# Attention with a routed expert layer on one core: the preparation reordered, with unread products on TensorE ahead of the first x

## The reference

```python
q, k, v = (split_heads(x @ W) for W in (Wq, Wk, Wv))
attn = softmax(q @ k.T * 128 ** -0.5) + bias        # bias[h, s, s]: rows of rel_table, clipped at both ends
out = (attn @ v) over the heads
x = layernorm(x + (norm(out, eps=1e-3) * gamma + beta))
w = softmax(top4((x @ hasher_w.T) @ keys.T))
x = layernorm(x + (x + scale * sum_k w_k * (silu(x @ values_down[k]) @ values_up[k])))
```

## Time and profile before

| what | us |
|---|---|
| median of 3 runs | 302.32 |
| lowest and highest | 301.48 and 304.64 |
| span of the profiled execution | 303.0 |
| PE busy in it | 280.6 (93%) |
| DVE, ACT, POOL busy | 235.2, 197.8, 129.1 |

### The profile page before, as it was taken

The page is one execution under the profiler, slowest core; times in us unless marked ns, Lnnn a source line. Parts: engine busy times, 40 slices in busy tenths (PEclk is TensorE's granted clock), DMA queues, the critical chain, the costliest instruction groups (busy, mean ns, idle before and its releaser), DMA issues.

```text
span 303.0 us, 10998 instructions
## 1 busy us (share of the span) xinstructions
PE 280.6 (93%) x4664; PEld 147.6 (49%) x4665; DVE 235.2 (78%) x517; ACT 197.8 (65%) x390; POOL 129.1 (43%) x212
## 2 busy tenths in 40 slices
PE   4969999999999989999999999999999999888991
PEld 3545434444444344444557554445566545375481
DVE  4755989998999978987787799977886863067854
ACT  3731389686777667789864876888566689921710
POOL 8576134110104651127556321288464033873641
PEclk9996999999999999999999999999999999999998
DMA  5566057355042302000403030006000000010011
GB/s 156 163 164 150 0 142 126 74 146 148 2 112 52 80 4 82 4 2 22 140 6 80 6 80 5 3 5 183 12 4 4 4 5 3 0 39 2 0 37 35
DMA packets 18574, 17.27 MB, mean 57 GB/s; under 512 B 6830, under 2 KB 16222, under 8 KB 18526
## 3 DMA queue, kind: packets, MB, share of 16 engines
q1 hardware_dynamic: 17856, 16.39, 21.3%
q10 hardware_dynamic: 670, 0.19, 0.3%
HBM read 12.18 MB, written 4.23 MB: 54 GB/s over the span
## 4 chain that ended last, share of the span: by engine, by line
PE 68%; DVE 11%; DMA 6%; ACT 5%; POOL 4%; issue 3%; SPq 1%; POOLq 0%; DVEq 0%
PE sm_ps L1208 16%; PE st_ps L1208 14%; PE ov_ps L1263 13%; PE mi_ps L1208 6%; PE si_ps L1208 5%; DVE neg_max L919 5%; DMA k_stack<-parts_dram 3%; ACT probs L773 2%; PE mi_ps L1270 1%; DVE stats L958 1%; POOL rstd L505 1%; ACT w_rows L675 1%; PE si_ps L1288 1%; PE st_ps L1435 1%; PE st_ps L1520 1%
## 5 line engine op out<-in xcount | busy, mean ns | idle before, releaser
L919 DVE TENSOR_REDUCE neg_max<-sm_ps 128x1 f32<-128x512 f32 x256 | 166.4, 686 | 31.3 <-PE sm_ps L1208 24.6
L773 ACT ACTIVATE probs<-st_ps 128x512 f32<-128x512 f32 x256 | 138.0, 608 | 33.8 <-PE st_ps L1208 33.8
L1208 PE MATMUL sm_ps<-k_stack,q_stack 96*32 96x512 bf16 x984 | 97.1, 383 | 2.8 <-DVE neg_max L919 2.1
L1208 PE MATMUL st_ps<-q_stack,k_stack 128*32 128x512 bf16 x1024 | 88.7, 380 | 0.2 <-ACT probs L773 0.2
L1263 PE MATMUL ov_ps<-probs,v_cur 128*32 128x256 f32 x1024 | 76.3, 378 | 0.0
L1208 PEld LDWEIGHTS sm_ps<-k_stack,q_stack 96*32 96x32 bf16 x984 | 26.3, 94 | 50.3 <-DVE neg_max L919 33.6
L519 POOL TENSOR_TENSOR hid<-hid,w_rows 128x512 f32<-128x512 f32 x27 | 34.2, 1281 | 30.8 <-ACT w_rows L675 30.7
L1263 PEld LDWEIGHTS ov_ps<-probs,v_cur 128*32 128x32 f32 x1024 | 31.6, 110 | 22.7 <-ACT probs L773 0.4
L1208 PEld LDWEIGHTS st_ps<-q_stack,k_stack 128*32 128x32 bf16 x1024 | 27.7, 96 | 28.4 <-ACT probs L773 9.2
L982 DVE SCALAR_TENSOR_TENSOR hid<-tanh_sb,mi_ps 128x512 f32<-128x512 f32 x24 | 16.3, 681 | 15.0 <-ACT tanh_sb L810 15.0
L1208 PE MATMUL mi_ps<-x_t,down_sb 128*32 128x512 f32 x192 | 25.1, 592 | 0.0
(11 more groups left out here) (183 smaller groups left out, 301.3 us busy)
## 6 DMA issues: line engine op xcount, KB each, us to landing
q_stack<-parts_dram SPq DMA_DIRECT2D x16, 288.0 KB
k_stack<-parts_dram SPq DMA_DIRECT2D x48, 96.0 KB
parts_dram<-parts SPq DMA_DIRECT2D x24, 128.0 KB, 2.4
x_sb<-L_attn_x SPq DMA_DIRECT2D x4, 256.0 KB, 4.7
out<-y_out SPq DMA_DIRECT2D x3, 256.0 KB, 2.3
down_sb<-L_ffn_values_down SPq DMA_DIRECT2D x1, 512.0 KB, 5.7
up_sb<-L_ffn_values_up SPq DMA_DIRECT2D x1, 512.0 KB, 8.0
rel_win<-rel_dram SPq DMA_DIRECT2D x1, 256.0 KB, 2.8
```

The source lines that it names most:

```text
L773: nc.scalar.activation(probs[:, u % 2, j, :], st_ps[:, score_bank(u * J + j), :], ACT.Exp, scale=SCORE_SCALE).then_inc(probs_ready, 1)
L919: nc.vector.tensor_reduce(neg_max[:, g % 2, col:col + 1], sm_ps[:, c % 2, :], AX.X, ALU.max, negate=True).then_inc(max_ready, 1)
L1208: i = nc.tensor.matmul(dst[n * TILE:(n + 1) * TILE], weights[:, n * TILE:(n + 1) * TILE], moving, **flags)
```

## The change

A new tile `warm` is filled by POOL's first instruction, ahead of `ident`. PE begins with products of it that nobody reads: five pairs (`row_halves`), each of two matmuls of 64 rows by 128 columns against 512 columns in float32r, one on the upper and one on the lower half of the rows and into two banks of `st_ps`, and two sets of four bf16 matmuls of 32 columns against 512 (`tiled`). The order is three pairs, then twice a set and a pair.

SP issues Wq and Wk behind x of batch 0, then x of 1, Wv, x of 2 and 3. The load of `rel_win` moves behind the six writes of batch 0's parts, and beta behind `load_shift(0, 0)`. ACT copies batch 1's turned x after the parts of batch 0. All four `add_beta` move to round 0, behind POOL's low parts of batch 3. PE makes q and k of batch 0 ahead of the turn of batch 1, v of batch 0 behind that turn, and the constant part of the bias, then the hasher's product, ahead of the first products for the maxima; the four of these that stood between the constant part's products are no longer there, so that two and twelve are made up to the end of the bias pieces and four more behind them.

```diff
--- before.py
+++ after.py
@@ -7,7 +7,7 @@
                                           hasher_w, keys, values_down, values_up, ffn_scale, out):
 
 
-    F32, BF16 = mybir.dt.float32, mybir.dt.bfloat16
+    F32, BF16, F32R = mybir.dt.float32, mybir.dt.bfloat16, mybir.dt.float32r
     ALU, ACT, AX = mybir.AluOpType, mybir.ActivationFunctionType, mybir.AxisListType
 
     B, S, E = x.shape
@@ -59,6 +59,7 @@
 
 
         ident, ident_bf = sb("ident", [P, P]), sb("ident_bf", [P, P], BF16)
+        warm = sb("warm", [P, P + S], F32R)
         minus_half = sb("minus_half", [P, C])
         wq_sb, wk_sb, wv_sb = sb("wq_sb", [P, E]), sb("wk_sb", [P, E]), sb("wv_sb", [P, E])
         gamma_sb, beta_sb = sb("gamma_sb", [P, E]), sb("beta_sb", [P, E])
@@ -118,6 +119,7 @@
         rel_dram = nc.dram_tensor("rel_dram", [NWIN + P // H, H], F32, kind="Internal").ap()
 
         waits_met = sem("waits_met")
+        warm_set = sem("warm_set")
         consts_made, stack_set, rows_cleared = sem("consts_made"), sem("stack_set"), sem("rows_cleared")
         x_loaded = [sem(f"x_loaded{b}") for b in range(B)]
         rows_loaded, beta_loaded = sem("rows_loaded"), sem("beta_loaded")
@@ -384,16 +386,12 @@
                 sp.dma_start(x_sb[:, b], x[b].rearrange("(c p) e -> p c e", p=P)).then_inc(x_loaded[b], 16)
 
             load_x(0)
-            load_x(1)
             sp.dma_start(wq_sb[:], w_q).then_inc(proj_loaded[0], 16)
             sp.dma_start(wk_sb[:], w_k).then_inc(proj_loaded[1], 16)
+            load_x(1)
+            sp.dma_start(wv_sb[:], w_v).then_inc(proj_loaded[2], 16)
             load_x(2)
             load_x(3)
-            sp.dma_start(wv_sb[:], w_v).then_inc(proj_loaded[2], 16)
-            sp.dma_start(beta_sb[:], bass.AP(beta.tensor, 0, [[0, P], [1, E]])).then_inc(beta_loaded, 16)
-            sp.wait_ge(rel_written, 32)
-            sp.dma_start(rel_win[:], bass.AP(rel_dram.tensor, 0, [[H, P], [H * P, NWIN // P], [1, P]])) \
-              .then_inc(rel_loaded, 16)
 
             def write_parts(b, *written):
 
@@ -408,6 +406,9 @@
                         sp.dma_start(rows[i], parts[:, b, a, i]).then_inc(written[a % len(written)], 16)
 
             write_parts(0, *first_written)
+            sp.wait_ge(rel_written, 32)
+            sp.dma_start(rel_win[:], bass.AP(rel_dram.tensor, 0, [[H, P], [H * P, NWIN // P], [1, P]])) \
+              .then_inc(rel_loaded, 16)
             sp.wait_ge(stack_set, 1)
             sp.wait_ge(rows_cleared, 1)
             sp.wait_ge(first_written[0], PARTS * 16)
@@ -417,6 +418,7 @@
             for g in range(1, G):
                 load_slice(0, g)
             load_shift(0, 0)
+            sp.dma_start(beta_sb[:], bass.AP(beta.tensor, 0, [[0, P], [1, E]])).then_inc(beta_loaded, 16)
             sp.dma_start(gamma_sb[:], bass.AP(gamma.tensor, 0, [[0, P], [1, E]])).then_inc(rows_loaded, 16)
             sp.dma_start(scale_sb[:], bass.AP(ffn_scale.tensor, 0, [[0, P], [1, 1]])).then_inc(rows_loaded, 16)
             write_parts(1, parts_written[1])
@@ -540,6 +542,7 @@
                         .then_inc(low_made, 1)
 
 
+            nc.gpsimd.memset(warm[:].bitcast(F32), 1.0).then_inc(warm_set, 1)
             nc.gpsimd.memset(ident[:], 0.0).then_inc(consts_made, 1)
             pool.wait_ge(consts_made, 1)
             nc.gpsimd.affine_select(out=ident[:], in_=ident[:], compare_op=ALU.not_equal, fill=1.0, base=0,
@@ -568,15 +571,11 @@
                 nc.gpsimd.tensor_tensor(x_sb[:, b], x_sb[:, b], beta_sb[:].unsqueeze(1).to_broadcast([P, C, E]),
                                         ALU.add).then_inc(xb_ready, 1)
 
-            pool.wait_ge(beta_loaded, 16)
-            add_beta(0)
-            add_beta(1)
             low_parts(1)
             low_parts(2)
             pool.wait_ge(v_copied, B)
             for g in range(G):
                 fetch_values(0, g)
-            add_beta(2)
             for i in range(PARTS):
                 rows = slice(i * NE, (i + 1) * NE)
                 pool.wait_ge(consts_made, 8)
@@ -585,12 +584,10 @@
                 nc.gpsimd.tensor_copy(spread[rows], ident[rows, rows].rearrange("r (j n) -> r j n", j=FJ).unsqueeze(3)
                                       .to_broadcast([NE, FJ, NJ, PD])).then_inc(spread_made, 1)
             pool.wait_ge(spread_made, PARTS)
-            add_beta(3)
             split_shift(0, 0)
             for n, a in enumerate((1, 0)):
                 pool.wait_ge(last_copied, n + 1)
                 nc.gpsimd.tensor_sub(resid[:, 1, a], resid[:, 1, a], parts[:, B - 1, a, 0, :]).then_inc(last_resid, 1)
-
             def round_(t, attention, experts, more, late):
                 f = t - 1
                 if attention and not is0(t):
@@ -605,6 +602,9 @@
                     split_shift(t, 1)
                 if is0(t):
                     low_parts(B - 1)
+                    pool.wait_ge(beta_loaded, 16)
+                    for b in range(B):
+                        add_beta(b)
                 if experts:
                     norm(f, "a", EPS_ATTENTION, z[:], z[:]).then_inc(pool_step, 1)
                     pool.wait_ge(pool_step, pool_at(f, "ascale"))
@@ -699,9 +699,9 @@
             nc.scalar.dma_start(rel_dram[LAST + 1:, :], bass.AP(rel_table.tensor, LAST * H,
                                                                 [[0, NWIN + P // H - LAST - 1], [1, H]])).then_inc(rel_written, 16)
             x_copy(0)
-            x_copy(1)
             high_parts(0)
             middle_parts(0)
+            x_copy(1)
             x_copy(2)
             x_copy(3)
             high_parts(1)
@@ -1397,17 +1397,29 @@
                 if kc == C - 1 and piece == pieces - 1:
                     i.then_inc(bias_mm, 1)
 
+            def row_halves():
+
+                for half in range(2):
+                    rows = slice(half * (P // 2), (half + 1) * (P // 2))
+                    nc.tensor.matmul(st_ps[:, half, :], warm[rows, 0:P], warm[rows, P:], start=True, stop=True)
+
+            pe.wait_ge(warm_set, 1)
+            for n in range(3):
+                row_halves()
+            for n in range(2):
+                tiled(st_ps[:, 2, :], warm[:].bitcast(BF16)[:, 0:P], warm[:].bitcast(BF16)[:, P:P + S], start=True, stop=True)
+                row_halves()
             pe.wait_ge(consts_made, 2)
             turn_x(0)
-            turn_x(1)
             pe.wait_ge(proj_loaded[0], 16)
             make_qk(0, 0)
             pe.wait_ge(proj_loaded[1], 16)
             make_qk(0, 1)
+            turn_x(1)
+            pe.wait_ge(proj_loaded[2], 16)
+            make_v(0)
             turn_x(2)
             turn_x(3)
-            pe.wait_ge(proj_loaded[2], 16)
-            make_v(0)
             make_qk(1, 0)
             make_qk(1, 1)
             make_v(1)
@@ -1423,11 +1435,7 @@
             make_v(3)
             pe.wait_ge(keys_loaded, 32)
             turn(si_ps[0:PD, 0:NE], keys_sb[:], ident[0:NE, 0:NE]).then_inc(table_mm, 1)
-            pe.wait_ge(xt_copied, B)
-            early_maxima(2)
-            pe.wait_ge(table_copied, 2)
-            nc.tensor.matmul(si_ps[:, 0:NE], hasher_sb[:], keys_t[:], start=True, stop=True).then_inc(table_mm, 1)
-
+            pe.wait_ge(table_copied, 1)
             pe.wait_ge(v_copied, B)
             pe.wait_ge(high_made, 6)
             pe.wait_ge(resid_made, 6)
@@ -1435,8 +1443,11 @@
                 i = nc.tensor.matmul(st_ps[:, 2, 0:CG * J * B * D], rel_t[:, LAST:LAST + P],
                                      v_all[:, kc, 0:CG * J].rearrange("p h b d -> p (h b d)"),
                                      start=(kc == 0), stop=(kc == C - 1))
-                early_maxima(1)
             i.then_inc(bias_mm, 1)
+            pe.wait_ge(table_copied, 2)
+            nc.tensor.matmul(si_ps[:, 0:NE], hasher_sb[:], keys_t[:], start=True, stop=True).then_inc(table_mm, 1)
+            pe.wait_ge(xt_copied, B)
+            early_maxima(2)
             for kc in range(C):
                 bias_product(CG, kc)
                 early_maxima(1, product=tiled)
```

## The result

The changed kernel took 305.11 us in the median of 11 runs (302.44 to 305.83), beside 302.32 (300.66 to 304.64) for 11 runs of the kernel before on the same chip: a ratio of 1.0066, 95% interval 1.0034 to 1.0099. It is slower by 0.3 to 1.0%; the forecast was 298.1.

The account below looks back on a forecast made before the run. It took a row of waits in the preparation, up to POOL's first split at 34.74, as the bound. Split 4.2 earlier, nothing lost in round 0: span 303.0 - 4.2 = 298.8, time 302.3 - 4.2 = 298.1 us, range 296.7 to 300.9.

Parts of the forecast that it names:

- the base: Starting point of the sum: the profile's span of 303.0, taken as 0.7 above the median of 302.32.
- split: POOL's first split, the mark on which everything up to the first scores hangs: 30.5 forecast for 34.74.
- Unread products: PE's start: seven steps end at 4.5, losing up to 0.4, and raise the clock (turn 0.65, q 0.86).
- Loads: SP's start: Wq, no longer queued behind batch 1's x, lands below 5.5; q at 5.8 to 6.85.
- Parts and writes: Batch 0's parts: SP's writes begin at 7.5 for 9.49, stacked loads land at 19.1, rel_win issued about 11.65.
- low-clock rival: Before the maxima: rel_win lands at 17 or later, PE idles, 1.2 GHz returns; 302.6, chance 0.04.
- PE to the first maximum: Idle 0.8 against 2.9, no clock fall; first product for the maxima at 20.1, reductions 0.62 apart.
- Sum: Whole kernel: 303.0 - 4.2 = 298.8 of span; time 302.3 - 4.2 = 298.1.
- 4.2 to be won: Gain at POOL's first split, 30.5 for 34.74: 0.9 from the earlier first reduction, the rest from five closing gaps.
- Round 0: Moved add_beta delays the second-group split 0.8 to 3.0; slack 1.65, 0 to 1.35 given back, nothing lost taken.
- Slower: Rival at PE's start: products overrun to 10.9 with the clock kept low; 3.5 slower, 305.8, chance 0.06.
- point of decision: In the slower rival: at the low clock, products ending from 7.4 on lose; below that a gain remains.

Follow-up runs that it names:

- e18: Kernel before plus five unread pairs of half-row float32r products ahead of PE's first turn, no narrow sets; 302.87 us, ratio 1.0022.
- e3: Kernel before plus only the change's unread products, their fill and PE's wait for it; 303.18 us, ratio 0.9988.
- e1: Changed kernel without the unread products and PE's wait for their fill; 302.49 us, ratio 0.9999 to the kernel before.
- e15: Changed kernel with the start's loads, turns and ACT copies in the old order and six whole bf16 unread products instead of its own; 301.54 us, ratio 0.9994.
- e5: Kernel before with only the constant part of the bias and the hasher's product moved ahead of all products for the maxima; 301.35 us, ratio 0.9947.
- e9: Kernel before, unchanged, run again for a second profile; 300.57 us, span 298.8.
- e10: Kernel before plus six whole bf16 unread products ahead of the first x and ten more in PE's idle time before the maxima; 300.59 us, ratio 0.9926.
- e7: Kernel before plus the fill and six whole bf16 unread products ahead of the first turn; 302.22 us, ratio 0.9968.
- e13: Kernel before plus six whole-row float32r unread products ahead of the first turn; 302.71 us, ratio 1.0029.
- e14: Kernel before plus six unread pairs of half-row bf16 products ahead of the first turn; 303.42 us, ratio 1.0045.

## Why the prediction was wrong, step by step

The sign was wrong, and the forecast is 7.0 us from the median. In the profile's terms: 2.5 from the base, 3.3 from a split at 33.81 instead of 30.5, 0.6 behind the split (268.9 for 268.3), and 0.7 by which after's median lies above its profile (305.11 and 304.45); rounded as they are, these come to 7.1.

- **Unread products** failed, on both counts. Size: "I take 4.5" became 5.53. That pairs overlap at about the bf16 pace was right: behind the first pair, which takes 0.59, e18's pairs start 0.43 apart, where 0.44 was taken. Most of the rest is the alternation: in after a set holds PE for 0.55, a pair ahead of a set for 0.56, and a pair behind a set for 0.72. Over the seven steps that is 4.12 for 3.1, and 0.9 of the 1.0 lies at the five changes of form. By the Trainium skill, TensorEngine Tiling, "Key Properties", a change of tiling mode drains TensorE; the prediction put an estimated 0.8 on this and left it out of its sum, and the 0.9 agrees with it. How much of that is the drain itself is not shown: the first pair has no change ahead of it and is 0.16 longer too. What they buy: "With it high, turn 0.65 and q 0.86" came out as 1.11 and 2.05. The sentence that was to guard against it, "some 3 us of f32 work were enough to raise the clock", took the old order's work for any work: in e3 and after TensorE worked on through 4.1 us of such products and was still at the lower clock behind them. The clock rose at 10.66 in after, at 10.26 in e1 without any.
- **Loads** held: with x turned at 3.95, q starts at 5.82 in e1, and what it waits for is ACT's copy, not Wq.
- **Parts and writes** failed with the clock and the overrun ahead of them: 10.13 for 7.5 in after, 8.52 in e1 without the products, 7.75 in e15 with an early clock. The same goes for rel_win: 14.88 for 11.65; it landed about 18.0 (14.88 and 3.1), just ahead of its turn at 18.09, so the low-clock rival's late rel_win did come, without costing an idle stretch.
- **PE to the first maximum**: 23.57 for 20.1 in after, 20.71 in e15. "Idle 0.8 against 2.9, so I expect no fall of the clock" was right, in after's profile and in all its runs (0.994 to 0.998); so was 0.62 between the reductions (0.60). What this is worth e5 shows: 1.3 us by the medians, 1.6 by the ratio, and nothing beside runs of before without the fall.
- **Sum** failed in "The span is 0.7 above the median of 302.32, inside the runs' scatter": span and time differ by about 1.8 in every run, so 298.8 of span would have been 300.6. The gap of 303.0 to the median was not scatter but the low clock of the earlier trace rows, which a median run has only in part and e9 not at all. Of the 4.2 to be won, an estimated 2.4 is what that execution had over a median run (34.74 for 32.3), and 3.8 what it had over e9 (30.98).
- **Round 0** failed at "nothing lost": 1.0 at the third split, inside the bound of 0 to 1.35. (Its slack of 1.65 goes by the chain, which shows PE's turn from 59.67; in the timeline that turn starts at 59.49, so it was 1.5.) That the 1.0 is back at the fourth split was not weighed, nor a wait for the shift rows.
- **The rivals.** *Slower* had the mechanism, an overrun with the clock kept low, and nearly the time (305.8), the latter by luck: the products ended at 5.53, not 10.9, and its point of decision, 7.4, came from a gain of 4.2. With the 1.8 that a median run had to give (32.3 - 30.5) that point is an estimated 4.5 + 1.8 - 1.3 = 5.0, and 5.53 lies beyond it.

Where the gain went: e15 shows the schedule nearly kept (split 30.94) and a time equal to before's. Of the 4.2, an estimated 2.4 was not there in a median run; 0.4 is the later split (30.94 for 30.5); round 0 keeps 0.8 (269.1 behind e15's split), as PE waits 0.8 for the shift rows. Some 0.6 us is left, and 0.4 is the difference of the medians. Beside an execution without the fall the new order had at most 0.5 to win: e9 has its split at 30.98 in the old one.

## What to carry to other kernels

Before working from one profile, set its own time against the runs: here the stretch to be removed was in that execution and missing in about half of the others. Unread work that is to raise TensorE's clock pays only if it ends before the first input lands, and has to be judged by the next instructions' durations; here it raised the clock without narrow sets between and not with them. Where the clock fell behind an idle stretch, ending that stretch (e10 by filling it, e5 by its order) went with no fall in any of their runs, while raising the clock earlier (e7, e13, e14, e18) did not prevent it.

## What the runs showed of the hardware

- Eighteen unread products from 1.41 to 5.53, pairs on half the rows and narrow sets by turns, left the next instructions at the lower clock (turn 1.11, Wq 1.87 to 2.05), while in seven profiles six whole ones, or five or six pairs, over a shorter stretch (1.4 to 3.9 or 4.1) were followed by the rise within the next two turns (4.20 to 5.77).
- With an earlier and busier start the later fall of the clock was more frequent: 34 of the 41 runs of e7, e13, e14 and e18 have a mean clock of 0.991 or less, 41 of the 79 runs of before beside them. Why is not shown.
- The windows' granted clock reads 1.00 from 0 to 18 in before and in after, though Wq took 1.86 and 2.05 there and 1.02 later. Before the first recorded change only durations show the level.
- PE's idle stretch ahead of the maxima was followed by 0.52 in one execution of before and by 1.00 in another (0.01 us of work in 2.9 and 0.56 in 3.0). Its length doesn't decide: PE's waits there were 2.97 in before, 2.61 in e3 and 2.43 in e13, with a fall, and 3.02 in e18 and 2.52 in e9, with none.
